# Routing in the last stage of a four-layer kernel: groups of four tiles in place of two

## The reference, cut to what matters

```python
S = L * N                                   # 2048 tokens
cap = int(CAP_FACTOR * S) // E              # 256
xf = x.reshape(S, D)
gates = softmax(xf @ wg)
idx = argmax(gates)
mask1 = one_hot(idx, E)
loc = sum((cumsum(mask1, 0) - 1.0) * mask1, -1)      # place among the tokens of the same expert
keep = loc < cap
slot = where(keep, idx * cap + loc, E * cap)
disp = zeros((E * cap, D)).at[slot].set(xf, mode='drop')
h = einsum('ecd,edf->ecf', disp.reshape(E, cap, D), w1) + b1[:, None, :]
y = (einsum('ecf,efd->ecd', h, w2) + b2[:, None, :]).reshape(E * cap, D)
out = where(keep[:, None], gate_val[:, None] * y[minimum(slot, E * cap - 1)], 0.0)
...
y1 = _ln(x + _mha(x, ...), ln1_g, ln1_b)
y2 = _ln(y1 + _moe(y1, wg, w1, b1, w2, b2), ln2_g, ln2_b)
```

## Time and profile before

| what | value |
|---|---|
| executions | 1690.9 us median of 3 (1688.8 to 1695.48) |
| the profiled execution, own time | 1689.8 us |
| its span, first to last instruction | 1688.1 us |
| mean granted TensorE clock | 0.94 of full |
| busy: PE, DVE, ACT, POOL | 89%, 64%, 26%, 27% |
| first operation of turn 0 on DVE | 1560.95 us |
| first scatter starts | 1583.77 us |
| last scatter starts | 1618.34 us |
| first transposes of the experts' rows | 1624.67 us |

### The profile page before, as it was taken

One profiled execution on the slowest core, in us unless ns is written; L12 is line 12 of the kernel. 1 busy time (PEld: TensorE's weight loads), 2 busy tenths in 40 slices (PEclk: granted clock), 3 DMA queues, 4 the chain that ended last, 5 costly groups with the idle time before them and its releaser, 6 DMA issues. The chain is left out here.

```text
span 1688.1 us, 26682 instructions
## 1 busy us (share of the span) xinstructions
PE 1504.5 (89%) x10586; PEld 924.9 (55%) x10586; DVE 1080.0 (64%) x3225; ACT 446.1 (26%) x687; POOL 462.6 (27%) x392
## 2 busy tenths in 40 slices
PE   7989789999999996898888889899998999698882
PEld 3447678888888884443333333344444558344761
DVE  1539898687877662487785667644783498423745
ACT  2332111111111000232333323321112477413232
POOL 0002323231415405066666575400000000000623
PEclk9999899999999997899999899999999999899865
DMA  8900000000000016365557664420142027000235
GB/s 355 228 9 1 2 2 8 2 9 2 9 2 9 3 32 224 141 196 165 172 164 266 192 208 142 131 112 1 37 163 63 14 83 240 0 7 1 70 124 107
DMA packets 86991, 155.92 MB, mean 92 GB/s; under 512 B 42075, under 2 KB 56532, under 8 KB 84308
## 3 DMA queue, kind: packets, MB, share of 16 engines
q1 hardware_dynamic: 64852, 82.91, 14.9%
q0 software_dynamic: 22016, 71.32, 14.2%
HBM read 141.62 MB, written 16.78 MB: 94 GB/s over the span
## 5 line engine op out<-in xcount | busy, mean ns | idle before, releaser
L514 PE MATMUL peer_ps_h<-all_x,layer_down 128*128 128x256 f32 x768 | 180.0, 388 | 0.0
L650 POOL TENSOR_TENSOR peer_bm<-peer_bm,peer_slots 128x512 f32<-128x512 f32 x36 | 109.0, 3028 | 244.7 <-DVE peer_bm L746 244.7
L1420 PE MATMUL skills_acc<-skills_hid,skills_w 128*128 128x512 f32 x256 | 129.7, 632 | 37.0 <-DVE skills_hid L1153 26.7
L514 PEld LDWEIGHTS peer_ps_h<-all_x,layer_down 128*128 128x128 f32 x768 | 144.3, 192 | 21.7 <-issue 1.9
L553 PE MATMUL peer_ps_o<-peer_hg,layer_up 128*128 128x256 f32 x640 | 142.3, 380 | 0.4 <-DVE peer_hg L778 0.4
L553 PEld LDWEIGHTS peer_ps_o<-peer_hg,layer_up 128*128 128x128 f32 x640 | 120.5, 190 | 20.4 <-issue 3.3
L595 ACT ACTIVATE peer_hg<-peer_ps_h 128x512 f32<-128x512 f32 x96 | 57.3, 597 | 274.6 <-PE peer_ps_h L514 274.6
L1473 PE MATMUL skills_ps_g<-all_x,skills_w 128*128 128x512 f32 x256 | 121.7, 598 | 0.0
L1473 PE MATMUL skills_ps_u<-all_x,skills_w 128*128 128x512 f32 x256 | 120.3, 592 | 0.0
L1420 PEld LDWEIGHTS skills_acc<-skills_hid,skills_w 128*128 128x128 f32 x256 | 50.2, 200 | 104.9 <-issue 65.0
L1487 ACT ACTIVATE skills_act_g<-skills_ps_g 128x512 f32<-128x512 f32 x96 | 56.3, 597 | 194.1 <-PE skills_ps_g L1473 170.3
(11 more groups left out here) (426 smaller groups left out, 2610.1 us busy)
## 6 DMA issues: line engine op xcount, KB each, us to landing
four_ring<-in_l_w SPq DMA_DIRECT2D x8, 1024.0 KB, 4.9
quant_w<-in_l_w SPq DMA_DIRECT2D x32, 256.0 KB, 4.6
all_early<-in_l_w SPq DMA_DIRECT2D x26, 256.0 KB, 3.8
four_skill<-in_skills SPq DMA_DIRECT2D x2, 3072.0 KB
skills_w<-in_skills SPq DMA_DIRECT2D x2, 3072.0 KB
layer_down<-in_down SPq DMA_DIRECT2D x1, 4096.0 KB, 25.5
layer_up<-in_up SPq DMA_DIRECT2D x1, 4096.0 KB, 35.2
expert_rows<-in_up SPq DMA_DIRECT2D x1, 4096.0 KB, 41.2
```

Of the source, the lines that this page charges most:

```text
L514: mm = pe.matmul(ps_h[group % 2][:, r, :], down[:, c, j * P:(j + 1) * P], g.x[:, c, bass.ds(i * PB, PB)], start=(c == 0), stop=(c == C - 1))
L650: pool.tensor_tensor(bm[c % RING][:], bm[c % RING][:], slots[half][:, 2, c * PAIRS:(c + 1) * PAIRS].unsqueeze(2).to_broadcast([P, PAIRS, WJ]),
L1420: mm = pe.matmul(acc[q % 2][c][:], w_down[s][:, m, c * P:(c + 1) * P], hid[j % 4][:], start=(s == 0 and m == 0), stop=(s == 2 and m == M2 ...
```

## The change

The routing steps work on groups of four tiles instead of two: groups 0 to 3 in place of pairs 0 to 7. All else stays in pairs. In the DVE list `choose` now stands in turns 4, 6, 8 and 10 and waits for the logits of two pairs; `count` stands in turns 5, 7, 9 and 11, and keeps its tile-by-tile running total, now over four tiles. PE's `count` stands in turns 5, 7, 9 and 11, each with the same two matmuls over 32 columns instead of 16. POOL issues four scatters in turns 5, 7, 9 and 11, each time after that turn's y1t if there is one. `ps_c` holds a group's counts in the same PSUM buffers as before.

```diff
@@ (tail, names)
+        GROUP = 4
...
-        ps_c = [x[:, 0:4 * E3].rearrange("p (k t e) -> p k t e", k=2, e=E3) for x in free[2:4]]
+        ps_c = [x[:, 0:2 * GROUP * E3].rearrange("p (k t e) -> p k t e", k=2, e=E3) for x in free[2:4]]
@@ (DVE)
-            def choose(p):
-                dve.wait_ge(l_done, p + 1)
-                ts = range(2 * p, 2 * p + 2)
+            def choose(r):
+                dve.wait_ge(l_done, (r + 1) * GROUP // 2)
+                ts, of = range(GROUP * r, GROUP * (r + 1)), slice(GROUP * r, GROUP * (r + 1))
                 then(*[dve.max(g8[:, t, :], logit[:, t, :]) for t in ts])
                 then(*[dve.max_index(gi[:, t, :], g8[:, t, :], logit[:, t, :]) for t in ts])
...
-            def count(p):
-                dve.wait_ge(counted, p + 1)
-                for t in range(2 * p, 2 * p + 2):
-                    then(dve.tensor_tensor(before[:, t + 1, :], ps_c[p % 2][:, 1, t % 2, :], before[:, t, :], ALU.add))
+            def count(r):
+                dve.wait_ge(counted, r + 1)
+                for t in range(GROUP * r, GROUP * (r + 1)):
+                    then(dve.tensor_tensor(before[:, t + 1, :], ps_c[r % 2][:, 1, t % GROUP, :], before[:, t, :], ALU.add))
...
-                if 0 <= i - 3 < NPAIR:
-                    choose(i - 3)
+                if i >= 4 and i % 2 == 0:
+                    choose((i - 4) // 2)
                 if i < NPAIR:
                     scale(i)
                 if i == 4:
                     dve.wait_ge(presets, 5)
-                if 0 <= i - 4 < NPAIR:
-                    count(i - 4)
+                if i >= 5 and i % 2 == 1:
+                    count((i - 5) // 2)
@@ (POOL)
-                if i >= 4:
-                    p = i - 4
-                    pool.wait_ge(vstep, marks["slot", p])
-                    pool.wait_ge(y1t_step, 2 * (p + 1))
-                    for t in range(2 * p, 2 * p + 2):
+                if i >= 5 and i % 2 == 1:
+                    r = (i - 5) // 2
+                    pool.wait_ge(vstep, marks["slot", r])
+                    pool.wait_ge(y1t_step, GROUP * (r + 1))
+                    for t in range(GROUP * r, GROUP * (r + 1)):
@@ (PE)
-            def count(p):
-                pe.wait_ge(vstep, marks["hot", p])
-                if p >= 2:
-                    pe.wait_ge(vstep, marks["counted", p - 2])
+            def count(r):
+                pe.wait_ge(vstep, marks["hot", r])
+                if r >= 2:
+                    pe.wait_ge(vstep, marks["counted", r - 2])
                 for k, ahead in enumerate((upto, ones)):
-                    mm = pe.matmul(ps_c[p % 2][:, k, :, :], ahead[:], hot[:, 2 * p:2 * p + 2, :], start=True, stop=True)
+                    mm = pe.matmul(ps_c[r % 2][:, k, :, :], ahead[:], hot[:, GROUP * r:GROUP * (r + 1), :], start=True, stop=True)
...
-                if 0 <= i - 4 < NPAIR:
-                    count(i - 4)
+                if i >= 5 and i % 2 == 1:
+                    count((i - 5) // 2)
```

More of the change, by code:

```diff
@@ L2116, in scale @@
                 dve.wait_ge(n_done, p + 1)
-            def choose(p):
-                dve.wait_ge(l_done, p + 1)
-                ts = range(2 * p, 2 * p + 2)
+            def choose(r):
+                dve.wait_ge(l_done, (r + 1) * GROUP // 2)
+                ts, of = range(GROUP * r, GROUP * (r + 1)), slice(GROUP * r, GROUP * (r + 1))
                 then(*[dve.max(g8[:, t, :], logit[:, t, :]) for t in ts])
                 then(*[dve.max_index(gi[:, t, :], g8[:, t, :], logit[:, t, :]) for t in ts])
[L2123 to L2126, removed]
-            def count(p):
-                dve.wait_ge(counted, p + 1)
-                for t in range(2 * p, 2 * p + 2):
-                    then(dve.tensor_tensor(before[:, t + 1, :], ps_c[p % 2][:, 1, t % 2, :], before[:, t, :], ALU.add))
-                of = slice(2 * p, 2 * p + 2)
-                then(dve.tensor_tensor(keep[:, of, :], ps_c[p % 2][:, 0, :, :], before[:, of, :], ALU.add))
-                marks["counted", p] = s.n
+                then(dve.tensor_copy(gif[:, of].unsqueeze(2), gi[:, of, 0:1]))
+                s.did(dve.tensor_tensor(hot[:, of, :], g.iota_a[:, 0:E3].unsqueeze(1).to_broadcast([P, GROUP, E3]),
+                                        gif[:, of].unsqueeze(2).to_broadcast([P, GROUP, E3]), ALU.is_equal))
+                marks["hot", r] = s.n
+            def count(r):
+                dve.wait_ge(counted, r + 1)
+                for t in range(GROUP * r, GROUP * (r + 1)):
+                    then(dve.tensor_tensor(before[:, t + 1, :], ps_c[r % 2][:, 1, t % GROUP, :], before[:, t, :], ALU.add))
+                of = slice(GROUP * r, GROUP * (r + 1))
+                then(dve.tensor_tensor(keep[:, of, :], ps_c[r % 2][:, 0, :, :], before[:, of, :], ALU.add))
+                marks["counted", r] = s.n
                 then(dve.scalar_tensor_tensor(out=hot[:, of, :], in0=keep[:, of, :], scalar=float(CAP), in1=hot[:, of, :],
@@ L2141, in count @@
                 s.did(dve.tensor_copy(slot[:, of], slot_f[:, of]))
-                marks["slot", p] = s.n
+                marks["slot", r] = s.n
             def weigh():
```

## The result

| | kernel before | changed kernel |
|---|---|---|
| median (7 runs each) | 1690.9 us | 1681.69 us |
| lowest to highest | 1686.9 to 1695.48 | 1679.13 to 1684.6 |
| profiled execution, own time | 1689.8 | 1681.16 |
| its span | 1688.1 | 1679.4 |

The ratio is 0.9946 with a 95% interval of 0.9931 to 0.9962: 9.2 us less, and by the interval 6.4 to 11.7. The forecast was 1683.5 us, 7.4 less; the range held the time, and the forecast lies inside the interval. In the terms of the chances the ratio itself lies a hair on the side of "faster by over 0.5%", which had 0.31, instead of "within 0.5%", which had 0.66; the interval takes in both, so the runs do not settle which of the two it is.

What follows compares the result with a forecast made beforehand. DVE was taken as the bound before 1606.69, POOL's scatter rate after. The last scatter would start at 1610.9 instead of 1618.34, so 1690.9 - 7.4 = 1683.5 us; 8-in-10 range 1679.5 to 1688.5.

Steps and rivals of the forecast that it cites:

- DVE's turns: DVE's normalisations in turns 3 to 7: fewer choices among them, the last ending at 1592.31.
- the loss of 1.3 us to products(4): DVE, turn 4: its measure must wait for PE's products(4), losing 1.3 us of the removed choice's gain.
- the middle value of 1.45 for the choice: DVE's choice over four tiles: 1.45 us, taken midway between bounds 0.98 and 1.96.
- The held count: DVE's first count, turn 5: held by POOL's y1t(5) until 1584.07, 3.30 us long as before.
- The first scatter's delay: POOL, group 0: the first scatter starts 0.85 us after its slots, as in the kernel before.
- the step: POOL's last 12 scatters, behind y1t(7): 11 steps of 1.29 us, 14.2 us in all.
- POOL the bound: Kernel before, from 1606.69 on: POOL's own scatter rate is the bound, with DVE just behind it.
- The tight slots: Slots of groups 2 and 3, behind exposed round trips: ready in time for POOL by 0.4 and 0.8 us.
- PE the bound: Rival, turns 4 to 7: a lower PE clock doubles products' time and turns wait up to 2.6 us; 1686.1 us, chance 0.13.
- the holds go away: Rival, DVE's counts: no hold by y1t, group 0's slots ready 1.6 us earlier; 1681.3 us, chance 0.16.

Runs made afterwards that it cites:

- e7: Changed kernel with `keep` and `spot` written to PSUM and ACT copying the logits ahead of the rows; ratio to the kernel before 0.9930.
- e13: e8 with `slot_f` in PSUM too; ratio to the kernel before 0.9912.
- e4: Changed kernel with group 0's four scatters issued after y1t(7) instead of ahead of y1t(6); turn 0 to last scatter 53.37 us, one execution.
- a0: The changed kernel run again, unaltered, in a later set; ratio to the kernel before 0.9941.
- e1: Kernel before with only the choices over four tiles, in turns 4, 6, 8, 10; counts and scatters stay in pairs; ratio to it 1.0031.
- e12: Changed kernel with only PE's count put back to the even turn, ahead of the next products; turn 0 to last scatter 60.88 us, one execution.
- e11: Changed kernel with counts and scatters in the turn of their choice on PE, DVE and POOL; turn 0 to last scatter 56.06 us, one execution.
- e8: e7 with the operations of y1t(6) and y1t(7) moved from POOL to DVE; ratio to the kernel before 0.9916.
- e10: e1 with both two-tile counts of a group, and their scatters, in the odd turn after the choice; turn 0 to last scatter 52.09 us, one execution.

## Why the prediction was right, point by point

The times of the changed kernel's trace, less the 0.34 us by which its stage began later, beside the prediction's:

| step | predicted | measured - 0.34 |
|---|---|---|
| normalisation of turn 3 ends | 1572.32 | 1572.32 |
| of turn 4 | 1578.69 | 1578.66 |
| of turn 5 | 1581.37 | 1581.30 |
| group 0's slots | 1584.71 | 1584.73 |
| first scatter | 1585.56 | 1585.03 |
| normalisation of turn 7 | 1592.31 | 1592.25 |
| y1t(7) ends | 1595.80 | 1595.23 |
| group 1's slots | 1596.40 | 1595.90 |
| fifth scatter | 1596.67 | 1596.18 |
| slots of groups 2 and 3 | 1601.2, 1605.9 | 1600.94, 1605.47 |
| last scatter | 1610.9 | 1610.13 |

- **DVE's turns: right**, to 0.1 us, with the loss of 1.3 us to products(4) (measured 1.34) and the middle value of 1.45 for the choice (1.40).
- **The held count: right in size**, and its cause is shown by e7 and e13: the same operations with one SBUF input run beside POOL's y1t in 0.17 to 0.19 us.
- **The first scatter's delay: mis-sized.** I carried 0.85 us over; it was 0.30, which is 0.5 of the 0.8 by which the last scatter beat the forecast. The other part is the step, 1.27 us instead of 1.29 over eleven of them (next point).
- **POOL the bound: right for the changed kernel**, by e4. For the kernel before I read the same from 1606.69 on, and there DVE was just ahead of it: to the end each pair's slots were ready 0.27 or 0.28 us ahead of its first scatter (the last four at 1609.02, 1611.58, 1614.14 and 1616.80, the scatters at 1609.30, 1611.86, 1614.42 and 1617.07). So the step of 1.29 held small waits for DVE, and with the slots there in time it is 1.27.
- **The tight slots: right that they were in time, by less than I put it.** Group 2's were ready at 1601.28 for a scatter that started at 1601.62, where 0.27 is the least between the two, so 0.07 us was to spare (0.4 predicted); group 3's had 0.6 (0.8 predicted). What I had not counted is the last operation of the count, a cast that ended only with the issue of the scatter beside it, in 0.41 us instead of 0.17 (POOL, then DVE):

```profile
1600.36 0.96 POOL L2251 DMA_INDIRECT slot_rows<-tail_y1t,tail_slot  x1 [0.30 <-issue]
1600.87 0.41 DVE L2142 CAST tail_slot<-tail_slot_f 128x4 uint32<-128x4 f32 x1
```

In a0 the same cast took 0.17 us and 0.3 us was to spare.

- **PE the bound: right that it does not happen, for a reason that I did not see.** I put it down to room in the turns. It is the place of PE's count: e1 and e12 show that with the choice over four tiles PE waits for it, unless the count stands a turn later. The change made both moves together. I listed the later turn as part of it and gave it no value; it is worth 11.7 us (e12). The lower clock, which I named as what could make PE the bound, was there in the kernel before: products(7) ran at a granted clock of 0.50 (1587.70 to 1593.00), and DVE did not wait for them.
- **The rival "the holds go away": wrong, though its time fits.** 1681.7 lies 1.8 us from my forecast and 0.4 from this rival's 1681.3. The trace decides: both holds are there (0.40 and 1.21 us), and the choice over four tiles took 1.40 us, not the 0.98 of two. Of that rival only the first scatter's extra delay vanished. That the time landed so near is chance: 0.86 us of it lie outside the stage's first half.
- **The 0.86 us behind the scatters** were in no step. In this trace PE's clock rose earlier in the experts' stage: the first eight expert matmuls took 3.78 us before and 3.21 now. In the other runs they took 2.60 to 3.78, and the stretch from the first transposes to the end 61.99 to 63.77 us, in no clear order with S (63.43 at S 57.39 and at 52.42, 61.99 at 53.82, 63.28 at 47.71). I take it for chance; what sets that moment was not tried.

## What to carry to other kernels

In a hand-ordered pipeline, making a step's batch larger delays its first result; look in every engine's list for what stands directly behind the instruction that waits for it, here the next products on PE, and move that waiting instruction back by as much. Where one engine issues a row of equal things at the end, the time is set by when its row starts without a gap, so the best batch is the one that still lets it begin early: four tiles here, not two and not eight. A short DVE operation that takes several times its usual time beside GpSimd work is held, and moving one operand to PSUM frees it, but look which operation inherits the hold.

## What the runs showed of the hardware

- A DVE operation with two SBUF inputs of 4 to 32 columns stood still until POOL's 128x512 multiplication or addition ended (up to 1.23 us instead of 0.18), and so did a cast from one SBUF tensor to another (0.89 us instead of 0.17 in the kernel before, 0.77 in e7, 1.28 in e11). With one input in PSUM the same operations took 0.17 to 0.19 us (e7, e13). The Trainium skill, "SBUF — State Buffer", section "Who interferes with whom", names both kinds, two-input operations and casts in a two-port mode, and says that a two-input operation is blocked only by a GpSimd instruction that reads SBUF. The traces agree on both kinds; that an instruction which only writes would not block, no run here shows.
- Under a scatter's issue the short two-input operations of the routing (up to 32 columns) took 0.16 to 0.23 us: they were not held. Casts and one-input operations from SBUF to SBUF were held there in the later part of the issue only: of 18 that began 0.51 to 0.71 us after its start, 17 ended within 0.04 us of its end, in 0.21 to 0.41 us; those that began up to 0.49 us after it took 0.17 to 0.21. One that read from PSUM (e13) was not held, 0.16 us. What sets that moment was not tried.
- The other way round, a scatter's issue grew from 0.96 to 1.33 us three times in e8 and e13, each time beside DVE's 128x512 multiplication and addition with two SBUF inputs. Why was not tried.
- The first scatter starts 0.85 us after its slots where the wait for `rows_written` stands directly ahead of it (kernel before, e1 and e11 alike), and 0.30 where y1t stands between (changed kernel, e10). What costs the 0.55 was not tried.
- A scatter of 128 rows costs POOL 1.27 us in a row of them (0.96 of issue, 0.30 to the next), 1.50 for the first of the stage and 1.31 for one behind y1t.
- In e12 and e1, after 2.8 us in which it had nothing to do, PE's products(5) ran at a granted clock of 0.51 to 0.54 of full, for the most part 1.2 GHz; the next pair's, directly behind them, ran at 2.4 GHz again. The same wait does not always end that way: in turn 6 of e11, after 2.81 us, four matmuls of 256 columns still took 1.11 us and the next four 1.92:

```profile
1522.59 0.41 PE L2300 MATMUL tail_free<-tail_hot,tail_upto 128*128 128x32 f32 x2 [2.81 <-DVE tail_hot L2125]
...
1523.06 1.11 PE L2272 MATMUL tail_ps_n<-layer_w_out,layer_o 128*128 128x256 f32 x4
...
1524.52 1.92 PE L2272 MATMUL tail_ps_n<-layer_w_out,layer_o 128*128 128x256 f32 x4
```
